# Who fetches the expert weights, and when c is fetched, at the start of a 32-sequence selective-scan and expert kernel

## The reference, cut to what matters

```
uo = x @ W_in.T;  u, o = split(uo)                      # hidden 256
u = silu(causal_conv(u, conv_w, 4 taps) + conv_b)
g = u @ W_gate.T;  delta_lo, b, c = split(g, [64, 16, 16])
delta = softplus(delta_lo @ W_delta.T + delta_bias);  A = -exp(A_log)
h_t = exp(A * delta_t) * h_(t-1) + (delta_t * u_t) * b_t      # 16 states per channel
y_t = sum over states of h_t * c_t
y = (y + D * u) * sigmoid(o) * o;   x = x + y @ W_out.T
# expert block, on layernorm(x): 8 experts of width 176, the best 2, and a shared one of width 352
x = x + sum_e combine_e * (silu(x @ w_gate_e) * (x @ w_up_e)) @ w_down_e + shared(x)
```

## Time and profile before

| | us |
|---|---|
| median of 3 runs (1227.39 to 1230.05) | 1228.54 |
| the profiled execution | 1223.18 |
| its span | 1220.2 |
| PE, DVE, ACT, POOL busy | 1120.7, 1067.7, 1004.2, 1067.8 |
| mean granted TensorE clock, share of full | 0.973 |

### The profile page before, as it was taken

How to read it: one execution, slowest core, us unless ns; L and a number is a source line. 1 busy time by engine, 2 the same in 40 slices (tenths; PEclk the granted TensorE clock), 3 DMA queues, 4 the chain that set the end, 5 groups by cost and what they waited for, 6 DMA issues and landing times. The chain is left out here.

```text
span 1220.2 us, 25690 instructions
## 1 busy us (share of the span) xinstructions
PE 1120.7 (92%) x9075; PEld 915.9 (75%) x9075; DVE 1067.7 (88%) x1702; ACT 1004.2 (82%) x2115; POOL 1067.8 (88%) x502
## 2 busy tenths in 40 slices
PE   4657999999999999999999999999999999998887
PEld 3435878777887787787877877887787788776676
DVE  3677999999999999999999999999989999999854
ACT  4877898888888988888898888888988888897742
POOL 3699999999999999999999999999989999999920
PEclk9668999999999999999999999999999999999999
DMA  5444434333443343234434433444342344434000
GB/s 143 127 109 105 110 80 114 99 81 93 110 110 108 86 114 88 81 105 110 110 89 105 104 83 86 110 109 110 85 111 79 85 108 112 108 76 109 5 6 9
DMA packets 71481, 115.05 MB, mean 94 GB/s; under 512 B 8173, under 2 KB 30394, under 8 KB 71354
## 3 DMA queue, kind: packets, MB, share of 16 engines
q1 hardware_dynamic: 67178, 110.71, 35.7%
q10 hardware_dynamic: 4176, 2.70, 0.8%
HBM read 41.04 MB, written 5.24 MB: 38 GB/s over the span
## 5 line engine op out<-in xcount | busy, mean ns | idle before, releaser
L414 POOL TENSOR_TENSOR inject<-rep,bc 128x1024 f32<-128x1024 f32 x256 | 604.9, 2386 | 28.6 <-DMA rep<-dd 28.6
L424 POOL TENSOR_TENSOR read<-state,bc 128x1024 f32<-128x1024 f32 x192 | 452.3, 2377 | 11.1 <-DVE state L696 10.0
L696 DVE TENSOR_TENSOR_SCAN state<-decay_ps,inject 128x1024 f32<-128x1024 f32 x192 | 431.9, 2278 | 21.6 <-ACT decay_ps L517 20.8
L517 ACT ACTIVATE decay_ps<-rep,neg_a 128x255 f32<-128x255 f32 x1024 | 425.5, 462 | 10.4 <-DVE state L696 3.6
L998 PE MATMUL acc_ps<-ffn_down,features 128*128 128x128 f32 (+1 forms) x1792 | 244.1, 281 | 0.5 <-DVE features L725 0.5
L998 PEld LDWEIGHTS acc_ps<-ffn_down,features 128*128 128x128 f32 (+1 forms) x1792 | 219.7, 191 | 23.3 <-issue 7.8
L964 PE MATMUL work_ps<-xn2T_part,ffn_gate 128*128 128x256 f32 x1344 | 217.8, 298 | 6.4 <-ACT g_silu L504 3.0
L504 ACT ACTIVATE g_silu<-work_ps 128x512 f32<-128x512 f32 x224 | 134.7, 601 | 102.7 <-PE work_ps L964 96.8
L964 PEld LDWEIGHTS work_ps<-xn2T_part,ffn_gate 128*128 128x128 f32 x1344 | 178.7, 191 | 51.6 <-ACT g_silu L504 22.5
L973 PE MATMUL work_ps<-xn2T_part,ffn_up 128*128 128x256 f32 x1344 | 192.2, 283 | 0.0
L717 DVE TENSOR_TENSOR features<-g_silu,work_ps 128x512 f32<-128x512 f32 x224 | 149.9, 682 | 45.2 <-PE work_ps L973 44.6
(11 more groups left out here) (134 smaller groups left out, 1248.6 us busy)
## 6 DMA issues: line engine op xcount, KB each, us to landing
rep<-dd SPq DMA_DIRECT2D x256, 256.0 KB, 4.7
bc<-bc_rows SPq DMA_DIRECT2D x64, 512.0 KB, 4.8
x_in<-in_L_attn_x_dram SPq DMA_DIRECT2D x32, 128.0 KB, 2.1
out_dram<-result SPq DMA_DIRECT2D x32, 128.0 KB, 1.8
bc_rows<-g_sb SPq DMA_DIRECT2D x32, 32.0 KB
state<-in_L_ffn_w_gate_dram ACTq DMA_DIRECT2D x1, 704.0 KB, 4.3
inject<-in_L_ffn_w_up_dram ACTq DMA_DIRECT2D x1, 704.0 KB, 6.5
ffn_down<-in_L_ffn_w_down_dram ACTq DMA_DIRECT2D x1, 704.0 KB, 8.4
```

What stands on the lines that cost most here:

```text
L414: pool.tensor_tensor(inject[:, at % RI], du_all, b_all, ALU.mult).then_inc(inject_done, 1)
L424: pool.tensor_tensor(read[:, at % RR], state[:, at % RS], c_all, ALU.mult).then_inc(read_done, 1)
L517: last = act.activation(decay_ps[:, at % 2, j, 1:T], rep[(HALVES * n + half) % RP][:, j, 0, 1:T], ACT.Exp, scale=neg_a[:, col:col + 1])
L696: dve.tensor_tensor_scan(to, decays, inject[:, at % RI].rearrange("p j t -> p (j t)"), 0.0, ALU.mult, ALU.add).then_inc(state_done, 1)
```

## The change

There are two edits. The seven `ffn_loads` are issued by SP behind the small weights, ahead of SP's loop, and no longer by ACT, which also loses its wait for `conv_loaded`. And for sequence 0 alone the transfer of c is issued between the four `rep` transfers of the first half and the four of the second, not right behind b; for all other sequences the order stays.

```diff
@@ block.sync
             for to, source in setup_loads:
                 sp.dma_start(to, source).then_inc(w_loaded, 16)
+            for to, source in ffn_loads:
+                sp.dma_start(to, source).then_inc(ffn_loaded, 16)
+
+            def spread_bc(n, which, landed):
+                rows_of = bc_dram[:, which, :, :].rearrange("s g t -> s (g t)")
+                sp.dma_start(bc[n % 2][:, which, :, :].rearrange("p g t -> p (g t)"),
+                             rows_of.unsqueeze(0).broadcast_to([CB, GS, SG * T])).then_inc(landed, 16)
...
-                    for which, landed in enumerate((b_in, c_in)):
-                        rows_of = bc_dram[:, which, :, :].rearrange("s g t -> s (g t)")
-                        sp.dma_start(bc[n % 2][:, which, :, :].rearrange("p g t -> p (g t)"),
-                                     rows_of.unsqueeze(0).broadcast_to([CB, GS, SG * T])).then_inc(landed, 16)
+                    spread_bc(n, 0, b_in)
+                    if k >= 0:
+                        spread_bc(n, 1, c_in)
...
+                        if k == -1 and half == 0:
+
+                            spread_bc(0, 1, c_in)
@@ block.scalar
             step(body, -3)
-            act.wait_ge(conv_loaded, 16 * len(conv_loads))
-            for to, source in ffn_loads:
-                act.dma_start(to, source).then_inc(ffn_loaded, 16)
             steps(body, -2)
```

## The result

| | before | changed |
|---|---|---|
| median of the first comparison, us | 1228.32 (4 runs, 1227.39 to 1230.05) | 1218.11 (4 runs, 1215.83 to 1218.88) |
| the profiled execution, us | 1223.18 | 1215.83 |
| its span, us | 1220.2 | 1213.8 |
| mean granted TensorE clock | 0.973 | 0.972 |

The ratio is 0.9923, with a 95% interval of 0.9899 to 0.9946. Two later series with the same kernel gave 0.9933 (0.9907 to 0.9960) and 0.9933 (0.9907 to 0.9959). Taken together, the medians are 1227.4 (72 runs) and 1218.9 (17 runs). So the change is faster by about 0.7%. Forecast was 1221.9, which is 0.9946 of the 1228.54 it started from: that is the upper end of the first interval and inside the two later ones.

A forecast was written before the change was run, and what follows sets the result against it. The prediction took the chain of waits up to about 55 us as what matters, the steps behind it only shifting. Edit 1's 4.9 and edit 2's 1.7 make 6.6 us: 1228.54 to 1221.9, range 1218.8 to 1226.6, forecast's chance 0.50.

The forecast's parts named there:

- ACT's stall gone: Start of kernel: without 7.41 us of issuing on ACT, `xn` comes near 5.0 and the convolution at 12.5.
- A_log in time: Before PE turns the small weights: A_log lands within 2.4 us of its issuing's end at 8.20, so PE needn't wait.
- that rival: A_log stays late: its 16-byte packets take 5.9 us, PE gains only 2.4 us; time 1224.4, chance 0.16.
- The full queue: Rival, chance 0.20: `bc_rows` waits behind expert weights on SP's queue, costing 1.3 us of the first `rep`; time 1222.9.
- Edit 2: Sequence 0's c behind the first half's `rep`: worth 1.7 us, by ACT's `u`, with the convolution limiting next.
- its first term: First `rep` of sequence 0 lands 2.0 us earlier without c ahead, between 0.6 and 2.4.
- Edit 1: Expert weights leave ACT: everything behind PE's convolution shifts 4.9 us earlier, between 2.4 and 5.1.
- The sum: Both edits at the start of the kernel together: 4.9 + 1.7 = 6.6 us.
- one for one: Premise: the engines' ring keeps its 35.3 us step, so an earlier start gives an equally earlier end.
- The gain unseen at the end: Rival, chance 0.10: two more long steps by the clock's whim take 4.4 of the 6.6 us; time 1226.3.
- The rule of the Trainium skill: Choice of issuing engine saves only issuing time, usually small; by it edit 1 is worth little and the sum 1.7.
- The slower rival: TensorE's low clock lasts into full steps from the fifth slice; 16 us of it gives 1232.3; chance 0.04.

The follow-up runs named there:

- e4: changed kernel, but SP issues the seven expert weights ahead of the eleven small ones; median 1226.75 us, ratio 0.9988.
- the first trace: profiled execution of the changed kernel from the first comparison, 1215.83 us; that comparison's median 1218.11 us, ratio 0.9923.
- e3: changed kernel run again unaltered, giving its second trace; median 1219.44 us, ratio 0.9933.
- e1: kernel before with only the expert weights moved to SP, c still right behind b; median 1220.23 us, ratio 0.9935.
- e11: changed kernel run a third time unaltered, giving its third trace; median 1219.36 us, ratio 0.9933.
- e7: changed kernel with the three transfers of w_down and sw_down issued behind sequence 0's rep, on their own semaphore; median 1217.47 us, ratio 0.9921.
- e12: the late w_down and sw_down version of the changed kernel run once more; median 1218.19 us, ratio 0.9934.
- e6: changed kernel with unread idle-time matmuls on TensorE, 20 ahead of turning the first weights and 32 in step -1; median 1221.37 us, ratio 0.9960.

## Why the prediction was right or wrong

**ACT's stall gone: right.** `xn` at 4.92 (5.0 was forecast), the transpose behind the turning, no wait for A_log, the convolution at 12.3 (12.5).

**A_log in time: right,** for the reason given. The 5.9 us of that rival were read from packets that had to share; alone they move at 354 a microsecond. e4 shows that the whole edit hung on this term, which the trace of before could not show.

**The full queue: absent in the first trace and the third, there in the second.** I had put it at 1.3 us; it took 1.2. That is near by luck: I had the traffic end at 20.6 and `bc_rows` at 19.3, and they came at about 19.2 and 16.70.

**Edit 2: right in mechanism, its first term too large.** I took 2.0 us for the landing of the first `rep`; by the means over the traces it is 1.2 to 1.5. The trace that I worked from was the slowest of the three with c ahead, at 13.0. For `u` I took 1.7. Alone, edit 2 gives 1.7 at the fourth gate, in one trace against two that differ by 1.5, and 3.7 in the medians; on top of edit 1 it shows 0.85. So 1.7 is not contradicted, and not confirmed to better than a microsecond. The convolution held `u` in two of the three traces of the changed kernel and the decays in the other, e3.

**Edit 1: a little too small.** I took 4.9, with 5.1 as its upper end if PE's turning and the transpose overlap. They do overlap, and the traces have 5.3 at the convolution in e1 (12.16 against 17.43): PE reached the small weights 0.4 sooner than in my sum. At `u` of the second sequence it is 5.2 against the mean of the two traces of before.

**The sum, and "one for one".** At the second `u` the three traces with both edits (34.36, 33.34, 34.59) lead the two of before (41.73, 40.11) by 6.8 us in the mean, where the sum said 6.6. At the fourth gate the lead is 7.3. The half microsecond between is no more than chance: from the second `u` to the fourth gate it takes 75.4 and 75.5 us in the kernel before, and 74.1, 76.5 and 74.3 in the changed one. The trace that was first at `u`, e3, was the last of the three at the fourth gate. So my premise that behind the start everything only shifts fits the medians of the steps, 35.0 to 35.1 in both kernels, but in a single trace the clock and the long steps move the gain by more than its error. The traces don't show the premise more exactly than that.

**The gain unseen at the end: its mechanism is there, in single traces.** I had named two long steps that take 4.4 us. In e3 and e11 the lead shrinks from 6.6 and 7.5 at the fourth gate to 4.4 and 2.0 at the last. The medians don't bear it out, with 7.1 to 10.2 us in three comparisons.

**What stays open.** The medians of all runs differ by 8.5 us, and the traces show 6.8 to 7.3 at the start; each series' interval is some 3 us wide on either side, and 6.6 lies inside two of them and at the edge of the first. The forecast of 1221.9 was built on the median of three runs, 1228.54, where all 72 runs of before have 1227.4, so the base was 1.1 us high. From that base the sum would give 1220.8, and the 1.9 us down to 1218.9 have no cause shown. That the change makes the long steps rarer is not it, by these few traces: they have more of them.

**The rule of the Trainium skill** on issuing engines ("DMA: Bandwidth & Descriptors", "Issuing engines are not separate DMA queues") would have made the edit worth little. Here the issuing was not "usually small": the stall was 7.41 us on ACT, beside some 12.4 us for the whole traffic, and the edit that removes it (with the small weights' late landing) gave 6.5 us at the fourth gate in e1. On the same page, the rule that one queue is consumed in order ("Queues, rings and completion order") agrees with e4, with the 3.1 us of the second trace and with the 3.0 of e7. These runs don't prove it, since sharing alone also delays: in the kernel before, A_log was late on a queue of its own.

**The slower rival** did not come up. A low clock as the full steps begin is in both kernels, at 0.50 from 102 to 110 us before and from 94 to 102 in the changed one, so it moved with the work and did not last longer.

## What to carry to other kernels

Look for a second cover behind each stall: here the issuing on ACT and the small weights' late landing ended within 0.2 to 0.5 us of each other (PE's waits for A_log in the two traces of before), and by the rows removing either alone would have given no more than that. e4, which frees ACT and leaves the small weights late, gave nothing. When transfers move to another queue, order them by who needs them first, and ask which small, late-issued transfer will find them still there: moving the bulk further back only changes which one that is. When a change is worth less than the spread of runs, compare stamps in several traces of each kernel; one pair can be off by 1 to 2 us.

## What the runs showed of the hardware

- Issuing seven transfers, 2.6 MB, held ACT for 7.4 us and SP for about 7 (8.24 to 15.04): the last two took 3.35 us of it.
- Packets of 16 bytes went at 354 a microsecond alone, about the pace of their issue, and 172 beside the large transfers.
- 32 KB written to DRAM took 1.9 us from issue to the issue that waits for it when nothing or only the tail of a transfer was in the way, and 3.1 (e3), 3.0 (e7) and 2.5 (e12) behind bulk transfers on the same queue.
- The profile's granted clock reads 1.00 at the start of both traces of the changed kernel, yet TensorE turned the same small weights at 0.21 us each in the one and 0.11 in the other. All ten other traces without added matmuls at the start are like the first. The windows from 11 to 12 us, the first trace and then the second:

```profile
11.00:12.00 1.00, 1.00 (x7) 1.00 (x6) 0.06 (x1) 0.00 (x0) 0.93 (x2) 1.00 1.11 369
```

```profile
11.00:12.00 1.00, 1.00 (x11) 1.00 (x10) 0.62 (x5) 0.66 (x5) 0.93 (x2) 1.00 1.11 366
```

  The Trainium skill's page "TensorE: Matmul & The Clock Gate", Part 1, says that the array runs at half clock out of idleness. The pace of the first trace agrees, the column at the start does not.
- Matmuls in a gap raise the pace of what follows directly (second convolution 3.12 us in e6 against 5.42), but the pace was lost again in the next wait of 3.7 us (clock 0.67 from 34 to 36 us and 0.50 from 36 to 38).
